# Projections of the last batch moved beside the first unit's row maxima, and key forming moved to GpSimd

## The reference

```
xn = (x - mean) / sqrt(var + 1e-5)
q = xn @ wq  (32 heads of 16);  k = xn @ wk;  v = xn @ wv    (one key head and value head of 16)
scores = q k^T / 4, causal;  probs = softmax(scores);  s = (probs v) @ wo
linear8bit(x, W, b): columns whose maximum over all tokens is > 3 are outliers, multiplied as they are;
    the others are rounded row by row to int8 steps (absmax/127), W too;  y = x_in_q @ W_q^T + x_out @ W^T + b
g = silu(linear8bit(linear8bit(xn, W1, b1), W2, b2))         (512 -> 2048 -> 512)
```

## Time and profile before

| | us |
|---|---|
| median of three runs | 787.97 |
| profiled execution, its own time | 785.56 |
| span of the profiled execution | 783.8 |
| TensorE busy | 749.8 (96%) |
| VectorE busy | 650.0 (83%) |
| ScalarE busy | 395.4 (50%) |
| GpSimd busy | 274.7 (35%) |

### The profile page before, as it was taken

How to read it: one execution, slowest core, us unless ns; L and a number is a source line. 1 busy time by engine, 2 the same in 40 slices (tenths; PEclk the granted TensorE clock), 3 DMA queues, 4 the chain that set the end, 5 groups by cost and what they waited for, 6 DMA issues and landing times. The chain is left out here.

```text
span 783.8 us, 11984 instructions
## 1 busy us (share of the span) xinstructions
PE 749.8 (96%) x4133; PEld 565.8 (72%) x4133; DVE 650.0 (83%) x1116; ACT 395.4 (50%) x671; POOL 274.7 (35%) x349
## 2 busy tenths in 40 slices
PE   5999999999999999999999999999997999999995
PEld 4878665556767666676578878878886888888884
DVE  7988999999999999896447568597859998599957
ACT  4454166777676776677834435354554433132212
POOL 7313135555555555555532212122100000027404
PEclk9999599999999999999999999999999999999998
DMA  8431303322333322325364677646324678527982
GB/s 268 152 108 54 82 18 86 84 80 77 94 105 84 84 85 83 83 83 150 111 240 161 151 241 212 188 99 164 84 57 144 237 232 251 169 81 246 321 292 107
DMA packets 93772, 110.71 MB, mean 141 GB/s; under 512 B 43136, under 2 KB 50320, under 8 KB 92176
## 3 DMA queue, kind: packets, MB, share of 16 engines
q1 hardware_dynamic: 93712, 109.95, 46.3%
HBM read 56.43 MB, written 40.37 MB: 124 GB/s over the span
## 5 line engine op out<-in xcount | busy, mean ns | idle before, releaser
L940 DVE TENSOR_REDUCE rowmax<-ps 128x2 f32<-128x512 f32 (+3 forms) x384 | 210.4, 592 | 19.4 <-PE ps L1017 17.8
L861 ACT ACTIVATE probs<-ps 128x512 f32<-128x512 f32 (+1 forms) x352 | 174.9, 559 | 70.0 <-PE ps L1030 68.6
L1017 PE MATMUL ps<-km,stack 128*128 128x256 f32 (+3 forms) x512 | 149.6, 347 | 2.2 <-PEq L195 1.9
L1030 PE MATMUL ps<-stack,ks 128*128 128x512 f32 (+1 forms) x352 | 131.8, 384 | 2.6 <-ACT probs L861 2.4
L1017 PEld LDWEIGHTS ps<-km,stack 128*128 128x128 f32 (+1 forms) x512 | 94.2, 197 | 43.2 <-DVE rowmax L940 23.7
L843 POOL TENSOR_SCALAR_AFFINE_SELECT probs<-probs 128x512 f32<-128x512 f32 x128 | 80.7, 638 | 75.8 <-ACT probs L861 74.3
L1887 PE MATMUL ps<-big_h 128*128 128x512 f32 x256 | 100.0, 390 | 2.0 <-DVE big_l L1703 1.6
L1889 PE MATMUL ps<-big_h,big_l 128*128 128x512 f32 x256 | 99.6, 389 | 0.0
L1888 PE MATMUL ps<-big_l,big_h 128*128 128x512 f32 x256 | 99.6, 389 | 0.0
L1043 PE MATMUL ps<-probs,vones 128*32 128x512 f32 (+3 forms) x1024 | 82.2, 439 | 0.2 <-POOL probs L843 0.2
L1030 PEld LDWEIGHTS ps<-stack,ks 128*128 128x128 f32 x352 | 66.4, 189 | 12.0 <-ACT probs L861 7.0
(11 more groups left out here) (227 smaller groups left out, 1370.4 us busy)
## 6 DMA issues: line engine op xcount, KB each, us to landing
stack<-big_h SPq DMA_DIRECT2D x128, 64.0 KB, 2.0
h_scratch<-hs SPq DMA_DIRECT2D x7, 1024.0 KB, 4.7
hload<-h_scratch SPq DMA_DIRECT2D x14, 512.0 KB, 5.2
xn_scratch<-xa SPq DMA_DIRECT2D x4, 1024.0 KB, 4.4
stack<-big_l SPq DMA_DIRECT2D x64, 64.0 KB, 2.0
xi<-xn_scratch SPq DMA_DIRECT2D x16, 256.0 KB, 2.7
xe_scratch<-xm SPq DMA_DIRECT2D x16, 256.0 KB, 2.3
w2n<-in_L_ffn_W_dram SPq DMA_DIRECT2D x4, 1024.0 KB, 6.5
```

Of the source, the lines that this page charges most:

```text
L861: nc.scalar.activation(probs[p][:, o:o + nh * w], ps[:, STB[n % NST], 0:nh * w], ACT.Exp).then_inc(s_exp, 1)
L940: nc.vector.tensor_reduce(dst, src, AX_X, ALU.max).then_inc(s_red, 1)
L1017: last = nc.tensor.matmul(dst, stack[u % 3][rows, hp, P * qt:P * (qt + 1)], km[rows, u // KT, p0:p0 + npar, keys], start=True, stop=True)
L1030: ins = nc.tensor.matmul(ps[:, STB[n % NST], 0:nh * w].rearrange("p (h q) -> p h q", h=nh), ks[:, u // KT, p, P * kt:P * (kt + 1)], stack[ ...
```

## The change

- Stage A ends after batch 2's last queries. The last batch is still normalised, transposed and split there, but its `kv`, `q` and `v` are left to stage B, and so are the `magic` matmuls. `xth`, `wqh`, `wql` and one `xtl` stay allocated until then.
- In stage B TensorE calls `late_products(g)` after `max_piece` in each step: in steps 0 to 29 two of the 60 remaining matmuls, the magic matmuls in step 0, the value transposes in step 18. They go to the banks that the scores and the values use only later. ScalarE copies them out twice (a whole float32 copy into SBUF, and the high part), and GpSimd, which cannot read PSUM, makes the low parts from the SBUF copies.
- GpSimd forms the keys of all batches (`score_keys`). The low part is subtracted in place in 32 partitions, so that one multiplication per p gives `km`, one addition gives `ks`.
- GpSimd makes the low part of `wo`, in four pieces of 512 columns; ScalarE makes the high part in four pieces. VectorE's column maxima take two banks at a time.
- The pieces of the first six units rotate over four banks (the three and `MISCB`), and the transposed maxima of the first five units take their turn in that ring. The counts of maxima and of projections become separate semaphores.

The diff, cut to its core:

```
@@ a_order @@
-        for g in range(B):
-            a_order += [("kv", g, 0), ("q", g, 0)]
-            if g + 1 < B:
-                a_order += [("q", g, k) for k in range(1, 3)]
-                a_order += [("t", g + 1, k) for k in range(KT)]
-                a_order += [("q", g, k) for k in range(3, KT)] + [("v", g, 0)]
...
-                a_order += [("q", g, k) for k in range(1, KT - 2)] + [("v", g, 0), ("b1", 0, 0)]
-                a_order += [("q", g, KT - 2), ("magic", 0, 0), ("q", g, KT - 1)]
+        for g in range(B - 1):
+            at = 3 if g + 2 < B else 2
+            a_order += [("kv", g, 0)] + [("q", g, k) for k in range(at)]
+            a_order += [("t", g + 1, k) for k in range(KT)]
+            if g + 2 < B:
+                a_order += [("q", g, 3), ("v", g, 0)]
+            else:
+                a_order += [("q", g, 2), ("v", g, 0), ("b1", 0, 0), ("q", g, 3)]
+        LAST = B - 1
+        late = [("magic", 0, 0), ("kv", LAST, 0), ("q", LAST, 0), ("q", LAST, 1), ("v", LAST, 0),
+                ("q", LAST, 2), ("q", LAST, 3)]
@@ new: keys on GpSimd @@
+        def score_keys(pool, g):
+            low = slice(4 * HD, 6 * HD)
+            pool.wait_ge(s_pah, high_at[("kv", g, 0)] + 1)
+            pool_steps[0] += 1
+            nc.gpsimd.tensor_tensor(kvh[low, :], kvf[low, :], kvh[low, :], ALU.subtract).then_inc(s_pool, 1)
+            pool.wait_ge(s_pool, pool_steps[0])
+            for p in range(2):
+                pool_steps[0] += 1
+                nc.gpsimd.tensor_tensor(km[:, g, p, :], kvh, cols[:, p:p + 1].broadcast_to([P, T]),
+                                        ALU.mult).then_inc(s_pool, 1)
+            pool.wait_ge(s_pool, pool_steps[0])
+            for p in range(2):
+                nc.gpsimd.tensor_tensor(ks[:, g, p, :], km[:, g, p, :].bitcast(F32),
+                                        cols[:, 2 + p:3 + p].broadcast_to([P, T]), ALU.add).then_inc(s_ks, 1)
+            pool.wait_ge(s_ks, 2 * (g + 1))
+            for p in range(2):
+                nc.gpsimd.tensor_copy(km[6 * HD:P, g, p, :].rearrange("r (j k) -> r j k", k=P),
+                                      later_k[6 * HD:P, :].rearrange("r (o k) -> r o k", o=1)
+                                      .broadcast_to([P - 6 * HD, QT, P])).then_inc(s_kz, 1)
+            pool.wait_ge(s_kz, 2 * (g + 1))
@@ GpSimd, stage A @@
+                for g in range(B - 1):
+                    score_keys(pool, g)
+                for k in range(KT):
+                    pool.wait_ge(s_wh, 2 + KT + k + 1)
+                    nc.gpsimd.tensor_tensor(wol[:, k, :], wo_in[:, k, :], woh[:, k, :].bitcast(F32),
+                                            ALU.subtract).then_inc(s_wl, 1)
@@ GpSimd, stage B, after fill_spare @@
+                score_keys(pool, LAST)
+                for k in range(KT):
+                    pool.wait_ge(s_pah, high_at[("q", LAST, k)] + 1)
+                    rows = slice(T * LAST, T * (LAST + 1))
+                    nc.gpsimd.tensor_tensor(big_l[:, k, rows], late_row(k), big_h[:, k, rows].bitcast(F32),
+                                            ALU.subtract).then_inc(s_paf, 1)
@@ stage B, ring of banks @@
+        LATE_AT = {("kv", LAST, 0): 0, ("q", LAST, 0): 6, ("q", LAST, 1): 12, ("v", LAST, 0): 18,
+                   ("q", LAST, 2): 18, ("q", LAST, 3): 24}
+        LATE_STEPS = 3 * KT // 2
+        for g in range(CH * U):
+            for use in [("p", g)] + ([("m", maximized(g, MAX_AT))] if 0 <= maximized(g, MAX_AT) < FOUR - 1 else []):
+                banks = MAXB + (MISCB,) if g < CH * FOUR else MAXB
+                bank = banks[len(ring) % len(banks)]
+                ring_at[use] = (bank, banks_at.get(bank))
@@ ScalarE, stage B @@
+                    if kind == "q":
+                        if k >= 2:
+                            act.wait_ge(s_paf, late_low_count(k - 2))
+                        nc.scalar.copy(late_row(k), full)
+                        nc.scalar.copy(big_h[:, k, T * LAST:T * (LAST + 1)], full).then_inc(s_pah, 1)
@@ TensorE, stage B @@
+                def late_products(g):
+                    if g == 0:
+                        pe.wait_ge(s_magc, 1)
...
+                    for use, at in LATE_AT.items():
...
+                        if kind in ("kv", "q") and at <= g < at + LATE_STEPS:
...
+                            for n in range(2 * (g - at), 2 * (g - at) + 2):
+                                if kind == "kv":
+                                    last = product(pe, dst, n, lambda k: wkvh[:, k, :], lambda k: wkvl[:, k, :],
+                                                   lambda k: xth[LAST % 2][:, k, :], lambda k: xtl[LAST % 2][:, k, :])
...
-                    if n >= NMAX:
-                        pe.wait_ge(s_red, n - NMAX + 1)
-                    bank, o = ps[:, MAXB[n % NMAX], :], 0
+                    bank, before = ring_at["p", n]
+                    ring_free(pe, before)
```

More of the change, by code:

```diff
@@ L193, in rows_of, with product @@
             return slice(QT * (g % 2), QT * (g % 2 + 1))
+        pool_steps = [0]
+        def score_keys(pool, g):
[18 more added lines that the diff above has]
+            pool.wait_ge(s_kz, 2 * (g + 1))
+        def product(pe, dst, n, lh, ll, rh, rl):
+            k, part = divmod(n, 3)
+            left, right = ((lh, rh), (lh, rl), (ll, rh))[part]
+            return nc.tensor.matmul(dst, left(k), right(k), start=(n == 0), stop=(n == 3 * KT - 1))
         with nc.Block() as block:
@@ L476, in three @@
                 def three(dst, lh, ll, rh, rl, ready=None, weights=None):
-                    for k in range(KT):
-                        if ready is not None:
-                            pe.wait_ge(s_tl, ready + k)
-                        if weights is not None:
-                            pe.wait_ge(s_wl, weights + k)
-                        nc.tensor.matmul(dst, lh(k), rh(k), start=(k == 0), stop=False)
-                        nc.tensor.matmul(dst, lh(k), rl(k), start=False, stop=False)
-                        last = nc.tensor.matmul(dst, ll(k), rh(k), start=False, stop=(k == KT - 1))
+                    for n in range(3 * KT):
+                        if n % 3 == 0 and ready is not None:
+                            pe.wait_ge(s_tl, ready + n // 3)
+                        if n % 3 == 0 and weights is not None:
+                            pe.wait_ge(s_wl, weights + n // 3)
+                        last = product(pe, dst, n, lh, ll, rh, rl)
                     return last
@@ L532, in _ @@
                         nc.tensor.transpose(dst[:, 0:FT], b1_in[:, :], ident[0:FT, 0:FT]).then_inc(s_pa, 1)
[L533 to L539 removed]
         prep.close()
[L543 removed]
+        until_scored.close()
         NP_ = NPAIR * sum(T - P * k for k in range(QT))
         probs = [sa(f"probs{p}", [P, NP_]) for p in range(2)]
+        stack += [sa(f"stack{i}", [P, NPAIR, T], F32R) for i in (1, 2)]
         P_OFF = [NPAIR * sum(T - P * j for j in range(k)) for k in range(QT)]
@@ L697, in block_layernorm_attention_ffn, with ring_free, projected_count, maxima_bank @@
         misc_at = {use: n for n, use in enumerate(misc)}
+        ring, ring_at, banks_at = [], {}, {}
+        for g in range(CH * U):
[3 more added lines that the diff above has]
+                ring_at[use] = (bank, banks_at.get(bank))
+                banks_at[bank] = use
+                ring.append(use)
+            if g == CH * FOUR - 1:
+                MISC_BEFORE = banks_at[MISCB]
+        def ring_free(engine, use):
+            if use:
+                kind, i = use
+                engine.wait_ge({"p": s_red, "m": s_mh}[kind], i + 1)
+        def projected_count(b, j):
+            return QT * b + j + 1
+        def maxima_bank(u):
+            return ring_at["m", u][0] if u < FOUR - 1 else MISCB
         def bank_of(use):
@@ L1000, in max_piece @@
                     n = CH * u + c
+                    if c == 0 and u == KT * LAST:
+                        pe.wait_ge(s_ks, 2 * B)
+                        pe.wait_ge(s_kz, 2 * B)
                     if c == 0 and u < 3:
```

192 lines of the change are left out of this document (113 added, 79 removed).

## The result

The changed kernel takes 774.78 us in the median of four runs (773.58 to 777.24), against 787.86 us (787.07 to 788.18) before: a ratio of 0.9837, 95% interval 0.9819 to 0.9855. The forecast was 774.3, range 771.0 to 779.0. The profiled executions lie at 773.78 and 785.56 us, 11.8 us apart, 1.9 us less than the sum of the forecast; the medians are 13.1 us apart.

What follows compares the result with a forecast made beforehand. TensorE was taken to bound stage A and units from 6 on, VectorE the first unit of stage B. Stage A 15.3, first unit -3.8 and ring 2.2 sum to 13.7 us gained: median 774.3 us, range 771.0 to 779.0.

Steps and rivals of the forecast that it cites:

- Stage A: Stage before the first piece: TensorE, its bound, loses the last batch's products; 15.3 us gained (14.0 to 15.6).
- The two waits: Stage A: TensorE's waits of 0.49 and 0.29 us for ScalarE vanish; 0.8 us gained (0 to 0.8).
- The stage's end: End of stage A: from TensorE's last product to the first piece, 2.2 us (2.0 to 3.0), GpSimd ending before VectorE.
- The first unit: Start of stage B: TensorE becomes the bound, first piece to first scores 23.0 us; a loss of 3.8 (3.0 to 4.8).
- the 3.0 us of rows 8 for the DMA: Before the first scores: the DMA's time in the profile of before, counted in the first unit's sum of 23.2 us.
- The ring: Units 1 to 5: a fourth bank for pieces removes VectorE's 0.5 us wait per unit; 2.2 us gained (0 to 2.6).
- The clock that falls and comes back: Rival, start of stage B: TensorE's clock halves after the gap, then returns; costs 1.8 us, giving 776.1; chance 0.22.
- The clock did not stay at half: Denies a rival: half clock through the first unit of stage B, giving 794.0 us, slower; chance 0.04.
- GpSimd was not late: Denies a rival: GpSimd's slowed list ends stage A, stage B starting 5.5 us later, giving 779.8; chance 0.04.
- ScalarE's copies of the late products: First unit: the forecast would be wrong if ScalarE's copies were found waiting for GpSimd; slack of 2 us and more.
- the ring gives nothing: Rival, units 1 to 5: the fourth bank brings no gain because ScalarE's banks hold TensorE, giving 776.5; chance 0.13.
- VectorE beside GpSimd: First unit: GpSimd's SBUF reads may delay three small VectorE instructions, some 3 x 1.0 us; sum same or up to 1 us worse.

Runs made afterwards that it cites:

- e8: Kernel before, with ScalarE's copy of a batch's keys no longer waiting for VectorE's copy of the previous batch's values; 787.25 us, ratio 0.9988.
- e2: Changed kernel with three banks instead of four for the pieces of all units; 776.24 us, ratio 0.9846 to the kernel before.
- e3: Kernel before with only the four rotating banks for the pieces in the first six units added; 787.13 us, ratio 0.9986.
- e9: Changed kernel with eight unused matmuls before the first piece and the first unit's maxima transposed one step earlier; 773.88 us, ratio 0.9818.
- e7: Changed kernel with the transposes of the row maxima one step earlier in all units; 779.84 us, ratio 0.9886 to the kernel before.
- e1: Changed kernel run again as it is, to see its spread; 774.51 us, ratio 0.9822 to the kernel before.
- e5: Changed kernel with three more VectorE reductions ahead of its last stage A subtraction, lengthening TensorE's gap; 779.15 us, ratio 0.9884.
- e6: Changed kernel with the low part of wo again one subtraction on VectorE instead of GpSimd; 777.65 us, ratio 0.9861.
- e11: Changed kernel with GpSimd's four subtractions for the low part of wo made twice; 779.87 us in one run.
- e10: Changed kernel with three more VectorE reductions ending stage A and seventeen unused matmuls filling most of TensorE's gap; 775.16 us, ratio 0.9835.

## Why the prediction was right

**Stage A.** Forecast 15.3 us, measured 15.1 (80.94 less 65.85). From first product to first piece it is 15.6 and 15.1 us in two executions; these differ by how long the first products run at the low rate. The two waits are gone, and e8 bears out the reason given, ScalarE's wait for VectorE's copy of the values. The stage's end is VectorE's, as forecast. From TensorE's last product (63.35 and one product of 0.23) to the first piece are 2.3 us; 2.2 was forecast.

**The first unit.** Forecast a loss of 3.8 us, measured 4.6, inside the bounds. TensorE is the bound in steps 0 to 29. Two sizes were off. The list up to the end of the maxima's transposes took 20.0 us, not 19.5, since 28 pieces cost 5.6 (5.4 forecast) and 56 products 13.25 (12.9). And the sum gave 23.2 us with the 3.0 us of rows 8 for the DMA, from which I took 0.2 on the guess that it would be shorter; it took 3.1.

**The ring.** Forecast 2.2 us, measured 1.4 between the profiles (unit 1 from first scores 0.4, unit 2 0.1, units 3 to 5 about 0.33 each), 1.7 by e2; the period of units 3 to 5 is 17.2 us, not 17.0. This is the term that was mis-sized: it took the whole 0.5 us wait as gain in each of 4.5 units. In units 3 to 5 the wait is gone, but VectorE's idle time fell only from 0.64 to 0.21 us a unit, and its busy time rose from 16.90 to 16.99, which leaves 0.34. In unit 1 the wait fell from 1.14 us to 0.81.

Together 15.1 - 4.6 + 1.4 = 11.9, against 11.8 between the profiled executions. The forecast's 13.7 was 1.9 too high there.

**Why the medians still came out.** They are 13.1 us apart. The profiled execution of before (785.56) was quicker than all its other runs, 787.07 and up, and 786.51 to 790.37 in later ones. e3 shows two causes that such runs can have. VectorE's delay of 1.8 us beside GpSimd's copy makes TensorE wait 0.7 us more in stage A, and it is the rule: 11 of the 13 profiled executions of all kernels here have it, the one of before and that of e9 do not. And the half clock lasts into unit 1 and costs 1.7 us there. The changed kernel shows no wait from the first, and in both its profiled executions the clock is at 1.0 through units 0 and 1. That these lay behind the other runs of before was not seen in a trace of them. So one profiled time is a poor basis for a sum moved to a median; the agreement with 774.78 to half a microsecond is luck in part: two errors that cancel.

**The rivals.** The clock that falls and comes back is real: e7 has it at a gap of 2.14 us, while the changed kernel, e1 and e2 went through 2.11 to 2.13 without. So it happens in some executions. It cost 1.6 us of unit 0 in e7 and 2.1 to 2.6 after the longer gaps of e5, e6 and e11; the forecast had 1.8. It is the likely reason for the changed kernel's runs at 775.8 to 777.2; their traces were not taken. The clock did not stay at half in any execution with dense work after the gap: it was back within 6 us of the first piece in e5, e6 and e11. GpSimd was not late, but has only 0.9 us to spare (e11); ScalarE's copies of the late products waited for TensorE alone, never for GpSimd. That the ring gives nothing is refuted by e2 and e3.

**VectorE beside GpSimd.** On VectorE's side the forecast looked for this in the first unit only. There VectorE's small instructions at the unit's end took 0.17 to 0.19 us; they fell into a pause of GpSimd (80.98 to 83.93), and there was no loss. Where it did strike is the end of stage A: the four instructions for the outlier marks took 1.71 us instead of 0.74 (e6). In the changed kernel this costs little, since VectorE's last subtraction started at 64.70 and could not have started before ScalarE's copy ended at 64.36.

## What to carry to other kernels

Work for an engine that is the bound belongs where it idles, and a stretch where a slow clock makes an engine look busy is such a place; price it by the start to start distance at full clock, not by busy time. When such a stretch becomes bound by TensorE, a gap of idleness ahead of it becomes dear: in this kernel a gap of 2.1 us in one profile of four, and gaps of 3.3, 4.3 and 6.5 us in the one profile of each, cost about 2 us more than they lasted, and useless matmuls in the gap prevented it (e10). Before a wait is put down to an edit, look whether the rest of the two executions is alike: in e8 a chance delay on VectorE hid two thirds of the gain. Pull a step of a pipeline forward only as far as its producer is ready in the steady state (e7).

## What the runs showed of the hardware

A VectorE instruction on 4 columns took 1.86 us in the changed kernel, started 0.07 us after a GpSimd copy of 1.89:

```profile
19.67 1.89 POOL L91 CAST stack<-later_q 32x2048 fp32r<-32x2048 f32 x1
```

```profile
19.74 1.86 DVE L412 TENSOR_SCALAR ve<-mv 128x4 f32<-128x4 f32 x1
```

It had taken 0.17 in the profiled execution of before (and takes 0.17 for the other batches), where the copy fell elsewhere. It is not the change that does it: in 11 of 13 profiled executions, e3 and e8 among them, some instruction of this chain took 1.74 to 1.86 us beside that copy. It stands in the chain to the next batch's rows. In the changed kernel it was hidden by 8 us of queries on TensorE; in e3 it was not.

GpSimd's subtraction of two tiles of 512 columns takes 1.25 to 1.29 us whether it works on 128 partitions (5.01 for four, L329 above) or on 32, as the in-place low part of the keys:

```profile
35.68 1.29 POOL L213 TENSOR_TENSOR projected_rows<-projected_rows 32x512 f32<-32x512 f32 x1 [5.98 <-ACT projected_rows L381]
```

For this the forecast had 1.0.
